# Inner pairs of four duos in one unit with samples on partitions, 101 such units a block, eight buffers for F products

## The reference

```python
e = jnp.stack([tbl_0[ids[:, 0]], ..., tbl_39[ids[:, 39]]], axis=1)   # (2048, 40, 64)
vi, vj = e[:, i_idx, :], e[:, j_idx, :]                              # 780 pairs
z = einsum('bpe,bpe->bp', einsum('bpd,pde->bpe', vi, W), vj)
h = concatenate([z, dense_ctx], axis=1)                              # 796
h = maximum(h @ W_top1 + b_top1, 0)                                  # 512
h = maximum(h @ W_top2 + b_top2, 0)                                  # 256
y = h @ W_top3
```

## Time and profile before

| | |
|---|---|
| median of 3 runs | 1236.45 us (1236.43 to 1236.52) |
| the profiled execution, its own time | 1235.92 us |
| its span (first to last instruction) | 1234.1 us |
| granted clock of TensorE | 1.00 throughout |
| busy: PE, DVE, ACT, POOL | 1216.8, 1004.4, 954.5, 781.1 us |

### The profile page before, as it was taken

One profiled execution on the slowest core, in us unless ns is written; L12 is line 12 of the kernel. 1 busy time (PEld: TensorE's weight loads), 2 busy tenths in 40 slices (PEclk: granted clock), 3 DMA queues, 4 the chain that ended last, 5 costly groups with the idle time before them and its releaser, 6 DMA issues.

```text
span 1234.1 us, 23139 instructions
## 1 busy us (share of the span) xinstructions
PE 1216.8 (99%) x5912; PEld 445.5 (36%) x5912; DVE 1004.4 (81%) x916; ACT 954.5 (77%) x7377; POOL 781.1 (63%) x1038
## 2 busy tenths in 40 slices
PE   7999999999999999999999999999999999999999
PEld 3333333333333333333333333333333333333333
DVE  7898999998787788898767868889787876788850
ACT  2174878998383889999688899999778899999841
POOL 8888883686655577777656666778766566423320
DMA  7332222222222222222222222222222222111100
GB/s 200 110 86 66 67 75 58 70 70 65 64 64 60 50 76 64 65 75 63 70 58 59 68 57 66 67 74 65 61 71 65 62 59 61 54 49 57 43 10 1
DMA packets 68477, 81.00 MB, mean 66 GB/s; under 512 B 15308, under 2 KB 46028, under 8 KB 68216
## 3 DMA queue, kind: packets, MB, share of 16 engines
q1 hardware_dynamic: 48752, 59.42, 16.1%
q0 software_dynamic: 19456, 19.96, 9.0%
q10 hardware_dynamic: 136, 0.14, 0.0%
HBM read 79.45 MB, written 0.01 MB: 64 GB/s over the span
## 4 chain that ended last, share of the span: by engine, by line
PE 95%; DVE 3%; issue 1%; ACT 1%; DMA 0%; SPq 0%; DVEq 0%
PE u_ps L940 35%; PE u_ps L936 23%; PE z_ps L957 19%; PE turn_ps L988 7%; PE turn_ps L908 3%; PE turn_ps L901 2%; PE turn_ps L998 2%; PE u_ps L988 2%; DVE acts L1051 1%; DVE fprod L1088 1%; PE u_ps L998 1%; PE turn_ps L974 1%; DVE rprod_A L1075 0%; DMA rows<-in_first_ids 0%; PE turn_ps L1007 0%
## 5 line engine op out<-in xcount | busy, mean ns | idle before, releaser
L1145 ACT ACTIVATE rprod_A<-rprod_A 128x64 f32<-128x64 f32 x3616 | 866.3, 242 | 105.2 <-DVE rprod_A L1075 102.7
L845 POOL DMA_INDIRECT rows<-in_tbl,ids_all x608 | 575.3, 946 | 274.1 <-issue 112.6
L1145 ACT ACTIVATION_READ_ACCUMULATOR rprod_A<-rprod_A 128x1 f32 x3616 | 680.3, 188 | 0.0
L1088 DVE TENSOR_TENSOR fprod<-u_ps,x 128x1024 f32<-128x1024 f32 x480 | 567.4, 1219 | 50.6 <-PE u_ps L940 50.0
L940 PE MATMUL u_ps<-x,wf_ring 64*128 64x512 f32 x1920 | 490.1, 607 | 3.6 <-ACT x L1132 1.8
L1075 DVE TENSOR_TENSOR rprod_A<-u_ps,rows 128x1024 f32<-128x1024 f32 x226 | 274.9, 1222 | 131.5 <-PE u_ps L936 131.5
L936 PE MATMUL u_ps<-wr_ring,x 64*128 64x512 f32 x1280 | 347.5, 612 | 0.7 <-DVE rprod_A L1075 0.5
L940 PEld LDWEIGHTS u_ps<-x,wf_ring 64*128 64x128 f32 x1920 | 175.1, 186 | 252.9 <-issue 186.7
L957 PE MATMUL z_ps<-fprod,ones 128*32 128x512 f32 x1920 | 251.9, 598 | 0.0
L865 POOL TENSOR_TENSOR rprod_P<-rprod_P 128x512 f32<-128x512 f32 (+4 forms) x245 | 148.5, 606 | 131.3 <-DVE rprod_P L1075 115.4
L936 PEld LDWEIGHTS u_ps<-wr_ring,x 64*128 64x128 f32 x1280 | 116.7, 186 | 171.2 <-issue 93.7
(11 more groups left out here) (37 smaller groups left out, 193.2 us busy)
## 6 DMA issues: line engine op xcount, KB each, us to landing
wf_ring<-in_w_standing SPq DMA_DIRECT2D x240, 128.0 KB
wr_ring<-in_w_moving SPq DMA_DIRECT2D x80, 256.0 KB
rows<-in_tbl,ids_all POOLq DMA_INDIRECT x608
mlp_sb<-in_mlp SPq DMA_DIRECT2D x1, 2308.0 KB, 9.6
mlp_sb<-in_tbl SPq DMA_DIRECT2D x6, 224.0 KB
rows<-in_first_ids SPq DMA_DIRECT2D x4, 256.0 KB, 5.8
rprod_P<-in_first_ids SPq DMA_DIRECT2D x4, 256.0 KB, 8.8
mlp_sb<-in_tbl SPq DMA_DIRECT2D x2, 280.0 KB
```

Source lines behind the costliest of these rows:

```text
L845: nc.gpsimd.indirect_dma_start(rows[:, v % ROW_SLOTS, s, par * DIM:(par + 1) * DIM], None, tables[f], bass.IndirectOffsetOnAxis(ap=ids_all ...
L1088: nc.vector.tensor_tensor(fprod[:, f % FPROD_SLOTS], u_ps[:, bank:bank + 2, :], other, ALU.mult).then_inc(prods_done, 1)
L1145: op = nc.scalar.activation(of[:, j, :], of[:, j, :], ACT.Copy, accum_out=sums_at(u, j, 1))
```

## The change

Inner pairs leave the F units. An I unit does the inner pairs of a quad's four duos: 16 small matmuls (2 duos per half of the rows, 4 subs, two halves) with 128 samples of `x` standing and 64 columns of weights moving. Its 1024 results per partition are multiplied with the odd fields' `rows` and summed over 64 neighbours like an R unit's, by the same three engines. `MOVED` becomes 24 chunks. A block now has 94 F, 96 R and 5 I units: 195, of which 101 have their samples on partitions. The last group of sums of a block has two F units, all chunks of `z_ps` use four strips, and the dense rows move to the last chunk of R's. z is still seven chunks: three from F, four from R and I. For quad 0 of block 0, whose rows were never gathered, PE turns the four duos of `x` back ("back") and ACT copies them into `rows`. There are eight `fprod` buffers instead of nine, a ring of two slots for I weights (64 KB a load), and some constants of the planner are others.

```diff
-MOVED = [0, 3, 4, 6, 7]
+MOVED = [0, 4, 5, 7, 8]
-WF_SLOTS, WR_SLOTS = 4, 2
+WF_SLOTS, WR_SLOTS, WI_SLOTS = 4, 2, 2
-FPROD_SLOTS = 9
+FPROD_SLOTS = 8
...
-STANDING = standing_units()
+STANDING = [("F", n, k) for n in range(DUOS) for k in range(MOVED[n // 4], n)]
-MOVING = [("R", c, s) for c in range(len(CHUNKS_R)) for s in range(SUBS)]
+MOVING = [unit for q in range(QUADS) for unit in
+          [("R", c, s) for c, (of, _) in enumerate(CHUNKS_R) if of == q for s in range(SUBS)] + [("I", q, 0)]]
-GROUPS = NF // GROUP
+GROUPS = -(-NF // GROUP)
-R_PAIRS = NC * FOLD
+R_PAIRS = NC * FOLD + DUOS
-DENSE_CHUNK, DENSE_ROW = (ZF - 1, 96) if Z_LAST <= 48 else (ZK - 1, R_PAIRS % P)
+STRIPS = 4
+DENSE_CHUNK, DENSE_ROW = ZK - 1, R_PAIRS % P
-def z_strips(k):
-    return 3 if k == ZF - 1 == DENSE_CHUNK else 4
...
+T_INNER = 1.75
-T_HOT, T_BUILD, T_TABLE, T_TABLES = 0.423, 0.35, 6.0, 1.6
-LEAD, LEAST, ROWS_LEAD = 4, 1, 4
+T_HOT, T_BUILD, T_TABLE, T_TABLES = 0.423, 0.535, 8.5, 1.6
+LEAD, LEAST, ROWS_LEAD = 6, 0, 5
-MLP_GAP, MLP_PACE = 6, 14
-AHEAD, BEHIND = 2, 10
-A_MOST, P_MOST = 1, 1
+MLP_GAP, MLP_PACE = 8, 12
+AHEAD, BEHIND = 2, 4
+BACK = 3
+A_MOST, P_MOST = 1.5, 1
...
+                elif back and turned >= HOT and (stall > STALL or u >= BACK) and self.bank_at <= soon:
+                    what = "back"
...
+            def load_inner(i):
+                if i >= WI_SLOTS:
+                    sp.wait_ge(mains_done, I_UNITS[i - WI_SLOTS] + 1)
+                sp.dma_start(wi_ring[:, i % WI_SLOTS, :], w_inner[i % QUADS]).then_inc(wi_in[i % WI_SLOTS], 16)
...
+                if kind == "I":
+                    for a, s in [(a, s) for a in range(2) for s in range(SUBS)]:
+                        to = slice((SUBS * a + s) * DIM, (SUBS * a + s + 1) * DIM)
+                        for half, on in enumerate(halves):
+                            op = pe.matmul(u_ps[:, bank + half, to],
+                                           x[on, x_slot(b, of[2 * half + a]), s * P:(s + 1) * P],
+                                           wi_ring[on, I_AT[u] % WI_SLOTS, a * DIM:(a + 1) * DIM],
+                                           start=True, stop=True)
...
+            def back(n):
+                ev = ("back", 0, n)
+                bank = bank_for(ev, TURN_AT[ev])
+                pe.wait_ge(turn_read, TURN_AT["duo", 0, n] + 1)
+                for s in range(SUBS):
+                    op = pe.transpose(bank[:, s * P:(s + 1) * P], x[:, x_slot(0, n), s * P:(s + 1) * P], ident[:])
+                op.then_inc(turned, 1)
...
             def sums(b, g):
-                for t in range(2 * GROUP * g, 2 * GROUP * (g + 1)):
+                for t in range(2 * GROUP * g, 2 * min(GROUP * (g + 1), NF)):
...
                     op = pe.matmul(z_ps[32 * strip:32 * strip + 32, :], ones[:, 30 - row:62 - row],
                                    fprod[:, f % FPROD_SLOTS, t % 2, :],
-                                   start=(r < strips), stop=(r >= tiles - strips))
+                                   start=(r < STRIPS), stop=(r >= tiles - STRIPS))
...
+                    if kind == "I":
+                        at = rows[:, first, 0, DIM:P]
+                        by = bass.AP(at.tensor, at.offset, [at.ap[0], [8 * P - DIM, 2], [P, 2 * SUBS], [1, DIM]])
+                        nc.vector.tensor_tensor(products_of(u).rearrange("p h (a d) -> p h a d", d=DIM),
+                                                u_ps[:, bank:bank + 2, :].rearrange("p h (a d) -> p h a d", d=DIM),
+                                                by, ALU.mult).then_inc(prods_done, 1)
+                        return
...
+            def back(n):
+                bank = bank_of(("back", 0, n))
+                nc.scalar.copy(rows[:, n, :, :].rearrange("p s c -> p (s c)"), bank[:, :]).then_inc(turn_read, 1)
```

More of the change, by code:

```diff
@@ L128, in z_place @@
     k, r = divmod(t, Z_TILES)
-    strips = z_strips(k)
-    return k, r % strips, 2 * (r // strips)
+    return k, r % STRIPS, 2 * (r // STRIPS)
 def tile_pairs(f, half):
[L135 to L139, removed]
+    _, n, k = STANDING[f]
     i, j = 2 * (DUOS - 1 - n) + half, 2 * (DUOS - 1 - k)
@@ L147, in moving_pair, with inner_pair, quad_of, stands @@
     return 2 * (DUOS - 1 - 4 * q - e // 2) + e % 2, 2 * (DUOS - 1 - k) + half
+def inner_pair(n):
+    return 2 * (DUOS - 1 - n), 2 * (DUOS - 1 - n) + 1
+def quad_of(kind, n):
+    return n if kind == "I" else CHUNKS_R[n][0]
+def stands(kind, n):
+    return list(range(4 * n, 4 * n + 4)) if kind == "I" else [CHUNKS_R[n][1]]
+def first_column(kind, n):
+    return FOLD * NC + 4 * n if kind == "I" else FOLD * n
+def units_until(c):
+    return 1 + max(r for r, (kind, n, _) in enumerate(MOVING) if first_column(kind, n) < P * (c + 1))
 def lay_standing(w):
     out = np.zeros((NF // HALF, P, HALF, P), np.float32)
-    for f, (kind, _, _) in enumerate(STANDING):
+    for f in range(NF):
         for half in range(2):
             for par, pair in enumerate(tile_pairs(f, half)):
[L158 to L161, removed]
+                out[f // HALF, half * DIM:(half + 1) * DIM, f % HALF,
+                    par * DIM:(par + 1) * DIM] = w[pair_index(*pair)]
     return out.reshape(NF // HALF, P, HALF * P)
@@ L171, in lay_moving, with lay_inner @@
     return out.reshape(NC, P, 8 * DIM)
+def lay_inner(w):
+    out = np.zeros((QUADS, P, 2, DIM), np.float32)
+    for q in range(QUADS):
+        for a in range(4):
+            one = w[pair_index(*inner_pair(4 * q + a))]
+            half = a // 2
+            out[q, half * DIM:(half + 1) * DIM, a % 2] = one.T if half else one
+    return out.reshape(QUADS, P, 2 * DIM)
 def lay_mlp(w1, b1, w2, b2, w3):
@@ L184, in lay_mlp @@
             lay1[row % P, ZF + row // P] = w1[pair_index(*moving_pair(c, a // 8, a % 8))]
+    for n in range(DUOS):
+        row = first_column("I", n // 4) + n % 4
+        lay1[row % P, ZF + row // P] = w1[pair_index(*inner_pair(n))]
     n_pairs = FIELDS * (FIELDS - 1) // 2
@@ L349, in take @@
         _, kind, n, _ = self.units[u]
-        if kind == "R":
-            b = self.units[u][0]
-            ready = max(ready, *(self.arrived[v] for v in range(DUOS * b + 4 * CHUNKS_R[n][0], DUOS * b + 4 * CHUNKS_R[n][0] + 4)))
+        if kind != "F":
+            first = DUOS * self.units[u][0] + 4 * quad_of(kind, n)
+            ready = max(ready, *(self.arrived[v] for v in range(first, first + 4)))
             self.owner_of(u, ready)
@@ L455, in build, with do_back @@
         self.built += 1
+    def do_back(self, n):
+        self.order.append(("back", 0, n))
+        self.pe_t = max(self.pe_t + self.turn_to("turn"), self.bank_at, self.copied[n]) + T_DUO
+        self.mode = "turn"
+        self.arrived[n] = self.bank_at = self.do_act(("copy", ("back", 0, n)), self.pe_t + LAG_PE, T_COPY)
     def do_sums(self, b, g):
@@ L526, in run @@
         self.done = {}
-        sums, mlp, last_step = [], [], -MLP_PACE
+        sums, mlp, last_step, back = [], [], -MLP_PACE, list(range(HOT))
         for b in range(NB):
@@ L719, in dlrm_tower @@
         wr_in = [sem(f"wr_in{s}") for s in range(WR_SLOTS)]
+        wi_in = [sem(f"wi_in{s}") for s in range(WI_SLOTS)]
         rows_free = sem("rows_free")
@@ L801, in _ @@
                 load_table(h)
+            for i in range(WI_SLOTS):
+                load_inner(i)
             for c in range(min(WR_SLOTS, NC)):
@@ L1015, in _ @@
                     duo(b, n)
+                elif what == "back":
+                    back(n)
                 elif what == "unit":
```

206 lines of the change are left out of this document (106 added, 100 removed).

## The result

The changed kernel takes 1202.08 us (median of 4 runs, 1201.28 to 1203.18), the kernel before 1236.44 beside it: a ratio of 0.9723 [0.9706, 0.9740]. The profiled execution took 1203.18 us with a span of 1201.4, 32.7 us shorter than before. Predicted were 1205 us, and a range of 1180 to 1236. Of the chips that the experiments ran on, two were slower for every kernel (before itself took 1334 us on one and 1361 on the other), so runs from there are read only as ratios to it and for what their traces show of single operations.

A forecast was written before the change was run, and what follows sets the result against it. PE was taken to set the time in blocks 1 to 3, PE and DVE together in block 0. From 1235.9 us, 3 more for block 0 and 34 less for blocks 1 to 3 gave 1205; range 1180 to 1236, likeliest part 1196 to 1218.

The forecast's parts named there:

- PE's terms: PE's work per block, priced by units, I units, sums, returns and turns: 17.3 us less a block, 66 us over all.
- Rival (c): I units load weights in series: 1222 us at 2.6 us each or 1240 at 3.5; chance 0.04 each.
- So block 0 becomes DVE's: Block 0: DVE's work of 266 us at a share of 94% to 97% takes 274 to 283 us, 275 taken.
- +3: Block 0's term in the forecast: 275 us, 3 more than before.
- a block 0 no shorter: Sign that the forecast is right: block 0 doesn't shorten; shorter by 10 us or more would show it wrong.
- Between the two points known: Blocks 1 to 3: with DVE at 88% to 90%, PE idles 2.5%, so each takes 281 us.
- DVE takes the rest: Sums over d that ACT and POOL leave go to DVE: 40, 29, 25, 24 by block, 118 in place of 45.
- the sum of 273.9: PE's priced work in a block of the changed kernel: 273.9 us in place of 291.2.
- (a): Rival: DVE's extra sums fit its gaps, PE alone sets the time in blocks 1 to 3 (1187) or all (1170); chance 0.20.
- (b): Rival: sums fall on DVE's queue ahead of products, PE waits for PSUM slots and the kernel ends slower, 1245 us; chance 0.10.
- (d): Rival: DVE's share costs more, or PE waits for gathers or ACT's copies in blocks 0 and 1: 1218 to 1234; chance 0.12.
- the edits that I costed at nothing: Eight product buffers, weight loads on SP's queue, rows held some 4 us longer, changed z and zr copies, four copies back: no cost.

The follow-up runs named there:

- e8: Kernel before with only the dense rows moved, so that the last chunk of F sums uses four strips; 1215.43 us, 0.9833 of the kernel before.
- e4: Changed kernel with an I unit's 16 matmuls reordered, eight of one half of the rows first, then the other eight; 1.0052 of before, on a slower chip.
- e10: Changed kernel with each of DVE's 102 sums cut to 2 of 64 elements, part of the computation left out; 1194.49 us.
- e12: Changed kernel with POOL given none of a block's last four sums, one more chunk in R units and a POOL backlog of two; 1197.32 us.
- e9: Changed kernel with the old MOVED, so 110 F, 80 R and 5 I units a block; 1208.40 us, 0.9777 of the kernel before.
- e1: Same edit as e8, four strips alone on the kernel before, run on a slower chip; 0.9933 of the kernel before.
- e7: Changed kernel again with no edit, beside the kernel before; 1201.28 us, 0.9715 of the kernel before.
- e2: Same edit as e9, changed kernel with the old MOVED, run on a slower chip; 1.0038 of the kernel before.
- e6: Same edit as e9, changed kernel with the old MOVED, run again on a slower chip; 1.0032 of the kernel before.

## Why the prediction was right

**Part of the nearness is luck.** The profiled execution, 1203.18 us, lies within 2 us of the forecast because misses cancel: block 0 was 8 us better, blocks 1 to 3 together 4 worse, start and tail 2 longer.

**PE's terms were right.** Units, sums, I units and strips came out as priced: 1.85 us for a group (forecast 1.85), 1.00 for the half group (0.99), 1.80 for an I unit (1.76). e8 gives 20.7 us for the strips (20.4), e4 the price of a load. One slip in the sum for block 0: before, it held five groups at 2.70 us and not six, so the strips save 4.25 us there and not 5.1 (e8: 4.0). Rival (c), I units in series (2.6 or 3.5 us each), is refuted by the timeline. In the other order of the loops a unit costs PE 1.0 us more, so even there 3.5 is too high.

**The split of the sums** was near: ACT 249 (forecast 234), DVE 102 (118), POOL 53 (52). The largest misses are in block 0, where ACT took 60 and not 54, and in block 3, where POOL took 22 and not 16, so that DVE had 16 sums and not 24. In block 0 I let ACT go only a little beyond what it did before, by its backlog; it went to 91%, from 75%.

**Block 0 was 8 us better than forecast.** The step "So block 0 becomes DVE's. At a share of 94% (as now) to 97% (close to no gap) it takes 274 to 283" held in its share, 97%, and failed in its work: ACT's six sums more left 33 to DVE and not 40, 7 x 1.13 = 8 us. So "+3" was -4.9, and the sign "a block 0 no shorter" was wrong.

**Blocks 1 to 3 were 4 us worse in sum, and unevenly.** Forecast were 11.5 us less for each; measured are 4.9, 11.6 and 13.6. Only block 2 lies in the 279 to 284 us that I named, and DVE's share in block 3, 87%, lies just under the 88% to 91%. Of PE's work 17.3 us a block went by my sum, so 12.4, 5.7 and 3.7 were given back. In block 1 some 6 us of the 12.4 are its border: 3.0 us of idle time and about 3 of half clock. Nothing in the earlier trace rows showed such a border, since the kernel before never stood long enough.

**The step that failed in its cause** is "Between the two points known (83% with 0.5% idle, 94% with 5.7%) I take 2.5% PE idle", together with "DVE takes the rest ... That is the price of the change". The size was near on the mean and in no single block: against the sum of 273.9 blocks 1 to 3 are 15.0, 7.6 and 2.7 us longer, 5.2%, 2.7% and 1.0%, together 3.0% where I took 2.5%. The cause wasn't what I said. I read DVE's share of a whole block and put the idle time down to DVE's extra sums; e10 takes them away and gains 6.8 us of the 31 given back over four blocks, more than half of it in block 0. The share is 79% while the network runs and 98.6% afterwards. There a group of sums with its duos and returns now comes every 195/23.5 = 8.3 units, before every 200/30 = 6.7. DVE's products alone need 8.3 x 1.13 = 9.4 us in a period in which PE has 8.3 x 0.86 + 1.85 + 0.2 + 0.85 x 0.79 = 9.9, before 7.5 of 8.5. Fewer sums on PE mean fewer pauses in which DVE catches up. That is worked out; e10 shows as much of it as that units still go at 1.13 us without DVE's sums. A run with shorter products wasn't made, so how much of the 31 us they hold, and how much ACT, which stands at 91% to 93% in every block and holds PE for 4.4 us at 228 us in e10, isn't settled.

**The rivals.** (a), PE alone (1170 or 1187): false, and false even for e10. (b), the sums fall on DVE (1245): false; it wanted 47 of them on DVE in a later block, and there were 28, 25 and 16. (d), 1218 to 1234: false as a time. It named gathers and ACT's copies; what block 1 shows is a wait of 2.29 us for a sum of POOL's, which no rival of the prediction named, and then 0.68 for a copy of ACT's. Of the edits that I costed at nothing, the weight loads show nowhere in the chain; nine buffers in place of eight, and the old constants with the new units, weren't tried.

## What to carry to other kernels

Read the shares of busy time by the parts of a loop that have different work, not by the whole loop: an engine at 88% of a block was at 79% and then at 98.6% of its parts, and the forecast needed the second. When work of one engine is cut, ask what it had been pacing: by the sum above, which no run tried alone, each group of sums that leaves PE is a pause in which DVE had caught up. When one engine is relieved, look at what it then runs into: e10 gained 6.8 us from 98.6 less on DVE, and PE stood for ACT and POOL instead. And price the plain part of a change by itself, since here 16 dense rows moved to another chunk brought 20.7 of 34.8 us.

## What the runs showed of the hardware

- After 3 us in which PE was mostly idle its granted clock went to 0.50 for some 7 us (0.77 in the microsecond from 315, 0.50 in the six from 316, 0.82 in the one from 322), and two units took 3.57 us, not 1.83. In e10 a wait of 4.1 us at 309 us did the same (clock 0.67 and then 0.50 in the next two windows of 4 us), and one of 4.4 us at 228. e12, whose wait there is 1.4 us with units before it, and e9, with waits of 2.5, kept 1.00. So at the changed kernel's border the low clock cost some 2.8 us on top of 3.0 us of idle time.
- Weight loads of 128 columns start 0.10 us apart on the same half of the rows (29 in 3.00 us with the last one's own 0.27) and 0.054 apart when the halves take turns (30 in 1.76 us with the last one's 0.19), even with a matmul of 64 columns behind each.
- Two chips ran every kernel slower, and the largest part of the lost time lay in block 0: e1's blocks are 65, 17, 21 and 6 us longer than e8's, the same kernel. e7's expectation, that all of it is lost in block 0, was too strong. The window from 100 to 150 us in e1, and under it the same for before on the first chip:

```profile
100.00:150.00 50.00, 29.10 (x120) 9.37 (x118) 22.88 (x19) 17.01 (x122) 44.21 (x70) 0.84 0.19 45
```

```profile
100.00:150.00 50.00, 48.52 (x253) 16.12 (x250) 44.12 (x40) 30.48 (x234) 44.22 (x71) 1.00 0.29 69
```

PE did 120 matmul records in place of 253 there, while POOL issued as many gathers (35, before 36). On such a chip the strips brought 0.65% and not 1.7%, and e2 and e6 were slower than before where e9 is 2.2% faster. Why wasn't settled.
